# State mixer and cross attention of a two-layer decoder in one loop of nine steps

## The reference

```python
# layer 0, state mixer
state = u @ W_b_rank @ W_b_state
state = _apply_butterfly(state, A_factors)     # five 2x2 factors, one for each bit of the 32 states
y = state @ W_c_rank @ W_c_model + D_vec * u
# layer 0, cross attention, one head
scores = einsum('bsd,bmd->bsm', hidden, memory) / 16, masked
out = softmax(scores) @ memory
# layer 0, FFN with ternary weights
w_dq = clip(round(w / mean|w|), -1, 1) * mean|w|      # gate, value and output weights
```

## Time and profile before

| | |
|---|---|
| time, median of 3 runs | 1252.36 us (1252.36 to 1252.71) |
| the profiled execution | 1250.75 us, of which its span is 1248.9 us |
| PE busy | 1060.5 us, 85% of the span |
| DVE busy | 894.2 us, 72% |
| ACT busy | 645.0 us, 52% |
| POOL busy | 324.4 us, 26% |
| mean granted clock of PE | 0.941 |

### The profile page before, as it was taken

How to read it: one execution, slowest core, us unless ns; L and a number is a source line. 1 busy time by engine, 2 the same in 40 slices (tenths; PEclk the granted TensorE clock), 3 DMA queues, 4 the chain that set the end, 5 groups by cost and what they waited for, 6 DMA issues and landing times.

```text
span 1248.9 us, 22083 instructions
## 1 busy us (share of the span) xinstructions
PE 1060.5 (85%) x6399; PEld 729.9 (58%) x6407; DVE 894.2 (72%) x2522; ACT 645.0 (52%) x2011; POOL 324.4 (26%) x496
## 2 busy tenths in 40 slices
PE   3676788689989967989999999899999998998396
PEld 1444345566666644556666666666656666665285
DVE  4576677487788765886867967778678678665375
ACT  0434777455555633655556545555565555552262
POOL 0212321211232121322313213223133132111456
PEclk9955999999999988989999999999999999999598
DMA  9501000112122000400000000000000000000731
GB/s 306 202 0 34 1 1 1 51 53 52 51 58 84 27 1 4 146 1 13 1 6 9 1 14 1 1 14 1 6 9 1 13 1 1 13 1 16 256 91 47
DMA packets 38795, 49.58 MB, mean 40 GB/s; under 512 B 5030, under 2 KB 29484, under 8 KB 38448
## 3 DMA queue, kind: packets, MB, share of 16 engines
q1 hardware_dynamic: 36400, 44.31, 11.9%
q0 software_dynamic: 2304, 4.24, 1.0%
HBM read 32.70 MB, written 14.78 MB: 38 GB/s over the span
## 4 chain that ended last, share of the span: by engine, by line
PE 37%; DVE 11%; issue 6%; POOL 3%; ACT 3%; DMA 0%; DVEq 0%; ACTq 0%; POOLq 0%
PE PS L1663 33%; POOL out_dram L1289 3%; DVE arena L746 2%; DVE arena L758 1%; DVE arena L722 1%; PE PS L2011 1%; PE PS L1988 1%; ACT arena L1505 1%; POOL tokens_dram L1265 1%; ACT arena L1514 1%; DVE arena L732 1%; DVE arena L728 1%; DVE small L780 0%; DVE early L655 0%; DVE early L650 0%
## 5 line engine op out<-in xcount | busy, mean ns | idle before, releaser
L1663 PE MATMUL PS<-EW,arena 128*128 128x128 f32 (+4 forms) x640 | 134.4, 341 | 18.0 <-DVE small L746 11.2
L1663 PE MATMUL PS<-early,arena 128*32 128x256 f32 (+6 forms) x856 | 105.1, 357 | 42.1 <-DVE early L612 23.7
L1663 PE MATMUL PS<-wq,EW 128*128 128x512 f32 x256 | 126.6, 617 | 12.6 <-DVE arena L722 12.3
L1203 POOL TENSOR_SCALAR small<-small 128x4 f32<-128x4 f32 x64 | 18.3, 286 | 427.4 <-ACT mask L1498 250.4
L1663 PEld LDWEIGHTS PS<-EW,arena 128*128 128x128 f32 x640 | 99.6, 193 | 48.9 <-issue 23.5
L746 DVE CUSTOM_DVE_ANT_0 arena<-PS,kmask 128x128 f32<-128x128 f32 (+3 forms) x256 | 92.4, 389 | 42.3 <-PE PS L1663 34.1
L1514 ACT ACTIVATE arena<-arena,small 128x128 f32<-128x128 f32 (+3 forms) x256 | 119.5, 471 | 1.3 <-DVE small L751 1.1
L1505 ACT ACTIVATE arena<-PS 128x512 f32<-128x512 f32 x64 | 38.2, 597 | 153.2 <-PE PS L1988 153.2
L1663 PE MATMUL PS<-wo,early 128*128 128x256 f32 x512 | 113.3, 380 | 2.5 <-DVE sinT L799 1.7
L1663 PEld LDWEIGHTS PS<-wo,early 128*128 128x128 f32 x512 | 97.2, 190 | 16.3 <-DVE sinT L799 2.1
L1663 PEld LDWEIGHTS PS<-early,arena 128*32 128x32 f32 (+3 forms) x864 | 49.8, 115 | 93.3 <-issue 45.5
(11 more groups left out here) (310 smaller groups left out, 2467.3 us busy)
## 6 DMA issues: line engine op xcount, KB each, us to landing
EW<-in_masksT_dram SPq DMA_DIRECT2D x32, 256.0 KB, 3.4
tokens_dram<-EW SPq DMA_DIRECT2D x1, 4160.0 KB, 14.9
arena<-tokens_dram SPq DMA_DIRECT2D x16, 260.0 KB, 3.0
results_dram<-EW SPq DMA_DIRECT2D x32, 128.0 KB, 3.2
EW<-results_dram SPq DMA_DIRECT2D x4, 1024.0 KB, 10.5
...
```

The costliest lines, as they stand in the source:

```text
L1663: return pe.matmul(dst, lhs, rhs, start=first, stop=last)
```

## The change

State mixer and cross attention become one loop, unrolled, of nine steps. In step n PE turns and multiplies batch n+1 of the mixer, turns and scores batch n of the cross attention, and turns the probabilities of batch n-1 and multiplies them by the context. Each of the two normalisations has its own buffers for statistics, result and turned copy (`aXN`, `aXT` and small tiles for the mixer), and is applied by ACT as `x * rstd + off`, where POOL makes `off` with two more instructions. Six banks of PSUM are used in place of four.

The butterfly becomes a 32 by 32 matrix `kron`, built by DVE in eleven small instructions from the factors, and multiplied by PE. SP issues the seven small loads first and then `x` batch by batch. The FFN weights are handled in six pieces of 1024 columns: magnitudes in steps 1 to 3 on ACT, the scale in step 4, rounding on ACT and limits on DVE from step 4 on, and the bias rows in step 4. The statistics of FFN batches 0 and 1 come at the end of steps 7 and 8. The first `gate` waits only for the gate weights' pieces.

```diff
+        wbs = sb("wbs", [R, NS])
+        factors = sb("factors", [NS, LV, 2, 2])
+        kron = sb("kron", [NS, 2, NS])
...
+            def head_stats(phase, b):
+
+                n = turn_of(phase, b)
+                if phase == MIX:
+                    dve.wait_ge(s_rows[b], 16)
+                else:
+                    dve.wait_ge(s_x, added(MIX, b))
+                if b > 0:
+                    dve.wait_ge(s_rs, turn_of(phase, b - 1) + 1)
+                for j in range(J):
+                    last = dve.bn_stats(h_st[phase][:, j, :], tokens(b, j))
+                last.then_inc(s_bn, 1)
+                dve.wait_ge(s_bn, n + 1)
+                for j in range(J):
+                    last = dve.bn_aggr(h_mv[phase][:, j, :], h_st[phase][:, j, :])
+                last.then_inc(s_mv, 1)
+
             dve.wait_ge(s_l0, 16 * 7)
-            const(dve.tensor_copy(identb[:, :], ident[:, :]), "identb")
             for lv in range(LV):
-                v = [fly[:, k, :].rearrange("r (a i c) -> r a i c", i=2, c=2 ** (LV - 1 - lv))
-                     for k in (lv % 2, (lv + 1) % 2)]
-                for o in range(2):
-                    f = 4 * lv + o
-                    const(dve.tensor_scalar(v[1][:, :, o, :], v[0][:, :, 0, :], factors[:, f:f + 1], None, ALU.mult))
-                    const(dve.scalar_tensor_tensor(v[1][:, :, o, :], v[0][:, :, 1, :], factors[:, f + 2:f + 3],
-                                                   v[1][:, :, o, :], ALU.mult, ALU.add), "fly")
+                const(dve.tensor_reduce(digits[:, lv, :],
+                                        ident[0:NS, 0:NS].rearrange("p (h k l) -> p k h l", k=2, l=2 ** (LV - 1 - lv)),
+                                        AX.XY, ALU.add))
+            const(dve.tensor_tensor(picked, factors[:, :, :, :], bc(digits.unsqueeze(2), [NS, LV, 2, 2]), ALU.mult))
+            const(dve.tensor_reduce(chosen, picked, AX.X, ALU.add))
+            last = chosen[:, LV - 1, :]
+            for n, lv in enumerate(range(LV - 2, -1, -1)):
+                k = 2 ** (n + 1)
+                grown = kron[:, n % 2, 0:2 * k].rearrange("p (i n) -> p i n", i=2)
+                const(dve.tensor_tensor(grown, bc(last.unsqueeze(1), [NS, 2, k]),
+                                        bc(chosen[:, lv, :].unsqueeze(2), [NS, 2, k]), ALU.mult))
+                last = kron[:, n % 2, 0:2 * k]
             dve.wait_ge(s_pp, 1)
+            const(dve.tensor_copy(c_fold[:, :], PS[0:NS, 2, 0:D]), "c_fold")
             const(dve.tensor_copy(b_fold[:, :], PS[0:NS, 1, 0:D]))
-            const(dve.tensor_copy(c_fold[:, :], PS[0:NS, 2, 0:D]), "folds")
-            ln_stats(MIX, 0)
-            ln_apply(MIX, 0)
+            head_stats(MIX, 0)
             dve.wait_ge(s_pp, 2)
+            const(dve.tensor_copy(turned_fold, PS[0:NS, 3, 0:D]), "folds")
+            head_stats(MIX, 1)
+            dve.wait_ge(s_pp, 3)
...
-            def mixer(b, nxt):
-                ln_stats(*nxt)
-                ln_apply(*nxt)
+                                               PS[:, 4 + c, c * P:(c + 1) * P], ALU.mult, ALU.add), "mix")
+
+            def mix_add(b):
+
                 dve.wait_ge(a_mm, b + 1)
-                dve.tensor_tensor(batch(b), batch(b), bank(1).rearrange("p (j d) -> p j d", j=J), ALU.add)\
+                dve.tensor_tensor(batch(b), batch(b), bank(2).rearrange("p (j d) -> p j d", j=J), ALU.add)\
                     .then_inc(s_x, 1)
-
-            over_batches(dve, MIX, mixer)
...
-            def clip(b, k):
-
-                w = wstage[:, ds(C * HID * k + C * HID // B * b, C * HID // B)]
-                n = 3 * b + k
-                dve.tensor_scalar(w, w, rgam[:, k:k + 1], 1.0, ALU.mult, ALU.min).then_inc(s_clip, 1)
-                dve.wait_ge(s_clip, 2 * n + 1)
-                dve.tensor_scalar(w, w, -1.0, MAGIC, ALU.max, ALU.add).then_inc(s_clip, 1)
...
-            def cross(b):
-                last = type(b) is int and b == B - 1
-                if not last:
-                    ln_apply(CROSS, b + 1)
+            def cross_max(b):
+
...
-                if type(b) is not int or b > 0:
-                    read_out(b - 1)
-                if not last:
-                    ln_stats(*((FFN, 0) if type(b) is int and b == B - 2 else (CROSS, b + 2)))
-                clip(b, 0)
-                if last:
-                    prepare(0, 0)
+
+            def cross_normalise(b):
...
-                for k in (1, 2):
-                    clip(b, k)
-
-            ln_stats(CROSS, 1)
-            cross(0)
-            bias_rows()
-            with dve.Fori(1, B - 2) as b:
-                cross(b)
-            cross(B - 2)
-            cross(B - 1)
-            ln_stats(FFN, 1)
-            read_out(B - 1)
+
+            def clip_low(i):
+
+                w, t = piece(i)
+                dve.wait_ge(s_clip, i + 1)
+                dve.tensor_scalar(t, w, MAGIC, -1.0, ALU.subtract, ALU.max).then_inc(s_tern, 1)
+
+            def clip_high(i):
+
+                w, t = piece(i)
+                dve.wait_ge(s_tern, 2 * i + 1)
+                dve.tensor_scalar(t, t, 1.0, None, ALU.min).then_inc(s_tern, 1)
+
+            def head(n):
+
+                if n < B:
+                    mix_add(n)
+                    head_stats(CROSS, n)
+                if n == 4:
+                    dve.wait_ge(s_abs, PIECES)
+                    const(dve.tensor_reduce(wsum[:, :], wpart[:, :, 0:2], AX.X, ALU.add), "wsum")
+                if n >= 1:
+                    cross_max(n - 1)
+                if n + 2 < B:
+                    head_stats(MIX, n + 2)
+                if n == 0:
+                    dve.wait_ge(s_l1, 48)
+                    const(dve.tensor_copy(mask[:, :, :], masku[:, :, :]))
+                    const(dve.tensor_scalar(mbias[:, :, :], mask[:, :, :], 1.0, -NEG, ALU.subtract, ALU.mult))
+                    const(dve.tensor_reduce(valid[:, :], mask[:, :, :], AX.X, ALU.max))
+                if n == 1:
+                    const(dve.tensor_copy(identb[:, :], ident[:, :]), "identb")
+                if n == 2:
+                    bias_patterns()
+                if n == 4:
+                    dve.wait_ge(s_pp, 4)
+                    const(dve.tensor_scalar(gam[:, :], PS[:, 7, 0:3], 1.0 / (D * HID), 1e-5, ALU.mult, ALU.max))
+                    const(dve.reciprocal(rgam[:, :], gam[:, :]), "gam")
+                if n == B:
+                    clip_low(5)
+                if n >= 1:
+                    cross_normalise(n - 1)
+                if n == 4:
+                    bias_rows()
+                for i in {4: (0,), 5: (1, 2), 6: (3,), 7: (4,)}.get(n, ()):
+                    clip_low(i)
+                    clip_high(i)
+                if n == B:
+                    clip_high(5)
+                    prepare(0, 0)
+                if n >= 1:
+                    read_out(n - 1)
+                if n == B - 1:
+                    ln_stats(FFN, 0)
+                if n == B:
+                    ln_stats(FFN, 1)
+
+            for n in range(B + 1):
+                head(n)
...
-            sp.dma_start(X[:, :, :, :], I["x"].rearrange("b (j p) d -> p b j d", p=P)).then_inc(s_lx, 16)
-            for dst, name in ((wbrT, "wbrT"), (wcrT, "wcrT"), (wcm, "wcm"), (ident, "ident")):
+            for dst, name in ((wbs, "wbs"), (wbrT, "wbrT"), (wcrT, "wcrT"), (wcm, "wcm"), (ident, "ident"), (dvec, "dvec")):
                 sp.dma_start(dst[:, :], I[name]).then_inc(s_l0, 16)
-            sp.dma_start(fly[:, 0, :], I["wbs"]).then_inc(s_l0, 16)
-            sp.dma_start(factors[:, :], I["factors"].partition_broadcast(R)).then_inc(s_l0, 16)
-            sp.dma_start(dvec[:, :], I["dvec"]).then_inc(s_l0, 16)
+            sp.dma_start(factors.rearrange("p l i k -> p (l i k)"), I["factors"].partition_broadcast(NS)).then_inc(s_l0, 16)
+            for b in range(B):
+                sp.dma_start(X[:, b, :, :], I["x"][b].rearrange("(j p) d -> p j d", p=P)).then_inc(s_rows[b], 16)
...
-            rstds(MIX, 0)
-            for phase in (MIX, CROSS):
-                over_batches(pool, phase, lambda b, nxt: rstds(*nxt))
+            def head_rstds(phase, b):
+
+                n = turn_of(phase, b)
+                k = phase
+                pool.wait_ge(s_mv, n + 1)
+                pool.tensor_scalar(h_ve[k], h_mv[k][:, :, 1], LN_EPS, None, ALU.add).then_inc(s_ve, 1)
+                pool.tensor_scalar(h_neg[k], h_mv[k][:, :, 0], -1.0, None, ALU.mult).then_inc(s_ve, 1)
+                pool.wait_ge(s_ve, 3 * n + 2)
+                if b > 0:
+                    pool.wait_ge(s_xn, turn_of(phase, b - 1) + 1)
+                pool.tensor_tensor(h_rstd[k], h_ve[k], halves[:, 0:J], ALU.pow).then_inc(s_ve, 1)
+                pool.wait_ge(s_ve, 3 * n + 3)
+                pool.tensor_tensor(h_off[k], h_neg[k], h_rstd[k], ALU.mult).then_inc(s_rs, 1)
+
+            head_rstds(MIX, 0)
+            head_rstds(MIX, 1)
+            for b in range(B):
```

(130 more changed lines are left out.)

158 lines of the change are left out of this document (87 added, 71 removed).

## The result

The changed kernel takes **1230.91 us** (median of 4; 1230.65 to 1231.92), the kernel before beside it 1252.53 (4; 1252.36 to 1254.42): ratio 0.9826, 95% interval [0.9808, 0.9843], 21.6 us less. The profiled execution took 1230.95, 19.8 less than the 1250.75 of before. All times inside a kernel are read from one profiled execution.

What follows compares the result with a forecast made beforehand. No engine was full; PE carried cross attention at 1.2 GHz, a ring the mixer. Start 18.2, step 1 to 34.6, steps 2 to 7 57.7, falls 5, end 8.5: `level_turn` at 105.8, 15.1 earlier; 1237.3 us by the median, range 1230 to 1247.

Steps and rivals of the forecast that it cites:

- first mixer product: Start of the kernel: small loads land at 7.2, product at 18.2 us against 26.11, 7.9 us earlier.
- steps 2 and 3: Common loop: two magnitude pieces, 3.0 us, delay ACT's copy; 8.6 us each, PE waiting 2.6 before the mixer product.
- steps 4 to 7: Rest of the common loop, with the weight work: 13.2, 10.6, 7.6 and 9.1 us.
- four falls besides: Clock falls after the 2.6 us waits in steps 2 to 5: four at 1.3 us on average, 5 us.
- from batch 6 to `level_turn`: End of the loop, output product of batch 6 to the FFN's first turn: 8.5 us, 2.0 lost.
- later stages: Everything behind `level_turn`: moved as it stands, no change in length.
- The ring: Common loop, one output product's end to the next: dependent chain sets an ordinary step at 7.6 us at 2.4 GHz.
- steps don't shorten: Rival, common loop: ring as long as both earlier rings, 12.2 us a step, nothing gained, 1250 to 1254; chance 0.05.
- Low clock: Rival: PE stays at 1.2 GHz through the loop and bounds it; gain 3.0, 1249.4 us; chance 0.18.
- Code fetch: Rival, nine unrolled bodies: fetch waits of 4.6 us on four engines in turn cost 18 to 25 us; chance 0.03.
- Steps 4 and 5: Loop steps with scale, bias rows, rounding and limits: `read_out` queued behind that work, 13.2 and 10.6 us.
- high-clock rival: Rival, common loop: no clock falls, gain 20, 1232 us; chance 0.12.

Runs made afterwards that it cites:

- the spread kernel: Changed kernel with bias rows and clips dealt out to steps 5 to 8, small product at the end of step 4, roundings a step later: 1222.11 us, ratio 0.9755.
- the two loops: Changed kernel's parts, but eight mixer batches ahead of eight cross-attention batches, TensorE's order within a cross batch as before: 1251.16 us, ratio 0.9979.
- with VectorE applying: Changed kernel with both loop normalisations applied by VectorE and POOL's two extra instructions gone: 1221.04 us, ratio 0.9752.
- the delayed kernel: Changed kernel with four copies of no use on VectorE ahead of the statistics of batch 0, a 1.8 us delay: 1226.37 us, ratio 0.9792.
- the filled kernel: Changed kernel with 128x256 products that nothing reads, into a free PSUM bank, where TensorE waits in the nine steps: 1227.50 us, ratio 0.9795.
- The delays: Changed kernel with four or eight copies of no use on VectorE ahead of batch 0's statistics: 1226.37 and 1228.56 us, ratios 0.9792 and 0.9806.

## Why the prediction held, and where it did not

Forecast were 1237.3 us in 1230 to 1247; 1230.9 is at the low edge. The steps, in us (measured in the profiled execution):

| step of the prediction | predicted | measured | what it adds |
|---|---|---|---|
| first mixer product | 18.2 | 16.45 | -1.8 |
| from it to the end of step 1 | 16.4 | 18.7 | +2.3 |
| steps 2 and 3 | 17.2 | 14.6 | -2.6 |
| steps 4 to 7 | 40.5 | 38.4 | -2.1 |
| four falls besides | 5.0 | in the rows above | -5.0 |
| from batch 6 to `level_turn` | 8.5 | 9.4 | +0.9 |
| later stages | 0 | +3.6 | +3.6 |

Up to `level_turn` that is -8.3, a gain of 15.1 + 8.3 = 23.4; less the 3.6, the 19.8 of the profiled executions.

- **Start.** Landing at 7.2 was 6.09, and the small instructions 2.2 us instead of 2.9. The order of the branches was right: ScalarE's ends last, with the table load on it. (My own terms put `mix` at 16.9, not 16.7; it is not on the path.)
- **The ring.** An ordinary step was forecast at 7.6 at 2.4 GHz; step 6 is 7.0, and so is step 5 of the spread kernel, which has no clock fall in it. The terms without the 0.5 for handovers add up to 7.05: the starts in the rows already held the handovers. That the common loop and not its parts carries the gain is shown by the two loops (21.4 of 23.4; how much of it by the clock is open), and the rival "steps don't shorten" is dead. In the ring ScalarE's application stood as 1.08 in place of 0.73. Of these 0.35 nothing is found in step 6 (7.0 against 6.9 with VectorE), and step 2 is shorter with ScalarE, since VectorE's queue is; the first product comes 0.4 later with it.
- **Low clock** had 1.2 GHz through the whole loop. It was there for about half of it (granted clock 0.77 from 16.45 to 97.53). **Code fetch** had four or more waits of 4.6 us in the new code; up to the head the timelines of TensorE, VectorE and ScalarE show a single wait without a releaser, 1.46 us on ScalarE at 93.01, just ahead of the FFN's application (0.54 in the delayed kernel).
- **Steps 2 and 3.** The mis-sized term is the pair of magnitudes, put at 3.0. The groups of ScalarE in the first 90 us have 1051 ns for one of 1024 values and 188 for the read of its sum, against the 1.24 that I took from the rounding (which is 1228 ns here too):

```profile
L1457 ACT ACTIVATE EW<-EW,magic,rgam 128x1024 f32<-128x1024 f32 x6 | 7.2, 1228 | 0.0
L1451 ACT ACTIVATE arena<-EW 128x1024 f32<-128x1024 f32 x6 | 6.3, 1051 | 0.3
...
L1451 ACT ACTIVATION_READ_ACCUMULATOR arena<-EW 128x1 f32 x6 | 1.1, 188 | 0.0
```

With 2.4 for the pair TensorE waits 1.79 us, not 2.6, and steps 2 and 3 have no falls.
- **Steps 4 and 5**, 13.2 and 10.6, were 13.1 and 10.0, for the reason given: the spread kernel makes 7.2 and 7.0 of them. But the 13.2 was meant without a fall, and 13.1 has one: the delayed kernel's 11.4 is the figure to compare, 1.8 below.
- **The clock.** I paid 5 us for four falls on top of steps that I had sized too long. By the filled kernel the falls up to step 7 cost 5.5 us or more, as the filling takes time too: 2.8 in step 1, where I had none, 1.3 and 1.4 in steps 4 and 7. So the sum was right by luck, and the places were wrong: of the four falls that I put into steps 2 to 5 one came there, in step 4. The high-clock rival gave 1232, nearer than the forecast, but not as it came out: the clock did fall, and the ring was shorter.
- **The end.** 8.5 was 9.4 here, and 8.4 in the delayed kernel and with VectorE applying. The 0.9 is no mistake of the sum but small waits of this execution (VectorE's 0.50 at 90.00, POOL's power of 1.17 instead of 0.9).
- **"The later stages are moved as they stand"** is the premise that failed, by 3.6 us. The delays show that it isn't the changed code: the same code behind `level_turn` takes 1126.9 us when the head is 0.4 later. Over the kernels here, all with the same code there, it runs from 1125.8 to 1135.3. In the changed kernel 2.2 of the 4.8 us against the delayed one are lost at 1033 us, to a wait that is 0.35 longer and the clock fall behind it. The clock alone doesn't rank the runs: behind `level_turn` it is at 1.2 GHz for 94.0 us in the changed kernel, 85.8 in the delayed and 86.9 before, but for 81.9 with VectorE applying, where the rest still took 1129.8. There the wait of 3.56 us at 873 came first and the fall followed. So two things move the rest: waits for which the profile shows no releaser, and the clock falls that come with some of them. Why they come where they do stays open.

The rule of the Trainium skill weighed in the prediction ("TensorE: Matmul & The Clock Gate", HAM oscillation) holds in part: the filled kernel shows that the clock stays up where the waits between the bursts are filled. Not each wait brings a fall: the same 1.79 us passed twice without one and not the third time, and in the delayed kernel the third time too. Several falls come behind waits of only 1.4 to 1.8 us (at 26.4, 53.7 and 1033.4 in the changed kernel), and what decides which of these waits brings one is not shown.
